# Turning attention probabilities by VectorE blocks and SBUF-to-SBUF DMAs instead of TensorE transposes

## The reference

```python
# layer 0
q, k, v = x @ Wq + bq, x @ Wk + bk, x @ Wv + bv          # split in 8 heads of 32
scores = einsum('bhnd,bhmd->bhnm', q, k) / sqrt(32)
attn = softmax(where(adj == 0, -inf, scores))
h = (attn @ v) @ Wo + bo
x1 = layernorm(h + x) * gamma0 + beta0
# layer 1
q, k, v = x1 @ Wq.T + bq, x1 @ Wk.T + bk, x1 @ Wv.T + bv
pros = softmax(where(adj == 0, -16384, q @ k.T))
z = v
for _ in range(4):
    z = 0.9 * (pros @ z) + 0.1 * v
out = layernorm(x1 + z) * gamma1 + beta1
```

## Time and profile before

| | us |
|---|---|
| runs of the kernel, median of 3 | 783.72 |
| lowest and highest | 782.49, 789.61 |
| the profiled execution, its time | 786.14 |
| its span, first to last instruction | 784.0 |
| PE busy | 754.1 (96%) |
| ACT busy | 665.7 (85%) |
| DVE busy | 637.1 (81%) |
| POOL busy | 547.8 (70%) |
| DMA, share of 16 engines (main queue) | 13.8% |

### The profile page before, as it was taken

How to read it: one execution, slowest core, us unless ns; L and a number is a source line. 1 busy time by engine, 2 the same in 40 slices (tenths; PEclk the granted TensorE clock), 3 DMA queues, 4 the chain that set the end, 5 groups by cost and what they waited for, 6 DMA issues and landing times.

```text
span 784.0 us, 32528 instructions
## 1 busy us (share of the span) xinstructions
PE 754.1 (96%) x11544; PEld 710.6 (91%) x11544; DVE 637.1 (81%) x3093; ACT 665.7 (85%) x2570; POOL 547.8 (70%) x417
## 2 busy tenths in 40 slices
PE   6889999999999999999999999999999999999974
PEld 6778999999999999999999999999999999998863
DVE  5778888888888888888888888888888888887765
ACT  4779998889889988988998898998889899899661
POOL 0336858666777777777787777787777778768774
PEclk9899999999999999999999999999999999999997
DMA  7101011010111101111111011111001111100002
GB/s 239 48 21 50 23 35 37 22 30 23 50 50 49 50 29 26 47 50 49 50 49 30 23 51 50 49 49 50 29 23 50 50 50 36 30 16 17 29 15 68
DMA packets 33245, 34.12 MB, mean 44 GB/s; under 512 B 2368, under 2 KB 28864, under 8 KB 33088
## 3 DMA queue, kind: packets, MB, share of 16 engines
q1 hardware_dynamic: 33088, 32.06, 13.8%
HBM read 23.67 MB, written 8.39 MB: 41 GB/s over the span
## 4 chain that ended last, share of the span: by engine, by line
PE 89%; DVE 3%; ACT 2%; issue 2%; DMA 1%; SPq 1%; POOL 1%; POOLq 0%; DVEq 0%; ACTq 0%
PE psF L342 23%; PE psF L411 18%; PE psF L351 16%; PE psF L401 15%; PE psS L391 9%; PE psF L456 7%; PE psF L436 2%; ACT ex L1011 2%; DMA w_raw<-in_w 1%; DVE sm L1400 1%; DMA out<-o_t 1%; SPq L284 0%; DVE o_t L1491 0%; DVE bst L1450 0%; POOL o_t L1927 0%
## 5 line engine op out<-in xcount | busy, mean ns | idle before, releaser
L1011 ACT ACTIVATE ex<-sm,nmax 128x128 f32<-128x128 f32 x1024 | 397.9, 397 | 3.3 <-DVE nmax L1400 2.3
L1859 POOL TENSOR_TENSOR pr<-ex,rec 128x1024 f32<-128x1024 f32 x128 | 245.3, 1918 | 101.1 <-DVE rec L1409 101.1
L1400 DVE CUSTOM_DVE_ANT_0 sm<-psS,mask 128x128 f32<-128x128 f32 x1024 | 228.3, 284 | 41.6 <-PE psS L391 41.4
L1011 ACT ACTIVATION_READ_ACCUMULATOR ex<-sm,nmax 128x1 f32 x1024 | 200.7, 196 | 0.0
L1022 ACT ACTIVATE pT<-psF 128x512 f32<-128x512 f32 x256 | 138.8, 596 | 34.5 <-PE psF L401 34.4
L401 PE MATMUL psF<-ident,pr 128*128 128x128 f32 x1024 | 137.8, 276 | 0.8 <-ACT pT L1022 0.5
L401 PEld LDWEIGHTS psF<-ident,pr 128*128 128x128 f32 x1024 | 112.7, 141 | 9.3 <-ACT pT L1022 0.9
L342 PE MATMUL psF<-xh,w_hi 128*128 128x256 f32 x512 | 112.6, 302 | 7.7 <-DVE w_lo L1339 5.7
L411 PE MATMUL psF<-pT,z 128*32 128x128 f32 x3072 | 103.1, 276 | 2.3 <-DVE z L1512 2.0
L342 PE MATMUL psF<-xh,w_lo 128*128 128x256 f32 x512 | 104.1, 285 | 0.0
L342 PE MATMUL psF<-xl,w_hi 128*128 128x256 f32 x512 | 103.6, 284 | 0.0
(11 more groups left out here) (76 smaller groups left out, 1425.7 us busy)
## 6 DMA issues: line engine op xcount, KB each, us to landing
xt_in<-in_x_t SPq DMA_DIRECT2D x32, 256.0 KB, 3.0
x_in<-in_x SPq DMA_DIRECT2D x32, 256.0 KB, 3.0
out<-o_t SPq DMA_DIRECT2D x30, 256.0 KB, 2.2
adj_in<-in_adj SPq DMA_DIRECT2D x32, 128.0 KB, 2.4
pT<-in_w SPq DMA_DIRECT2D x4, 256.0 KB, 4.0
row<-in_rows SPq DMA_DIRECT2D x1, 768.0 KB, 6.8
w_raw<-in_w SPq DMA_DIRECT2D x3, 256.0 KB, 7.0
out<-o_t SPq DMA_DIRECT2D x4, 128.0 KB, 1.7
```

The costliest lines, as they stand in the source:

```text
L1011: e = nc.scalar.activation(ex[l][:, b, h, :], sm[l][:, b, h, :], ACT.Exp, scale=-1.0, bias=nmax[l][:, b, h:h + 1], accum_out=tot[l][:, b, ...
L1400: last = nc.vector.tensor_tensor_reduce(sm[l][:, b, h, :], psS[:, o:o + N], mask[p.parity][:, b, :], -1.0, BIG, ALU.add, ALU.min, nmax[l][ ...
L1859: nc.gpsimd.tensor_tensor(pr[l][:, b, :, :], ex[l][:, b, :, :], rec[l][:, b, :].unsqueeze(2).broadcast_to([128, H, N]), ALU.mult).then_inc ...
```

## The change

DVE turns the probabilities in blocks of 32x32 (`turn_blocks`: one instruction for each layer and graph, 128 x 1024 each, from `ex` to the new tile `blk`). That leaves each block transposed in place, on the partitions of its row block; SP then carries block (i, j) to the partitions of column block j with 16 DMAs for each layer and pair (`move_blocks`), SBUF to SBUF. PE's `turn_probs`, ACT's `save_pT` and the tile `pr` are gone. POOL multiplies in place in `ex`.

With it: `save_q` and `save_k` go from DVE to ACT, as two ACTIVATE instructions of 128 x 256 each because ACT takes a bias of one column; hop 0's copy goes from DVE to ACT; the mask is kept four deep; the PSUM banks are dealt to other uses; `spread` reads the turned probabilities in runs of 32 elements. The orders of all engines are new, and the unrolled step runs from t = 9 to 31. POOL has waits on DVE's progress between its calls (`beside`), which guard no data.

```diff
-        mask = [sb(f"mask{i}", [128, 2, N]) for i in range(2)]
+        mask = [sb(f"mask{i}", [128, 2, N]) for i in range(4)]
-        pr = [sb(f"pr{l}", [128, 2, H, N]) for l in range(2)]
+        blk = [sb(f"blk{l}", [128, 2, NB, H, BS]) for l in range(2)]
-        pT0 = sb("pT0", [128, 2, H, N])
-        pT1 = [sb(f"pT1_{i}", [128, 2, H, N]) for i in range(2)]
+        pT0 = sb("pT0", [128, 2, NB, H, BS])
+        pT1 = [sb(f"pT1_{i}", [128, 2, NB, H, BS]) for i in range(2)]
...
+            def move_blocks(l, p):
+                if p.real:
+                    for b in range(2):
+                        sp.wait_ge(blk_s[l][b].sem, blk_s[l][b].at(p))
+                    if l:
+                        sp.wait_ge(hr[NUM_HOP - 1].sem, hr[NUM_HOP - 1].at(p - 2))
+                    else:
+                        sp.wait_ge(avr.sem, avr.at(p - 1))
+                    for i in range(NB):
+                        for j in range(NB):
+                            sp.dma_start(pT[l][p.parity][BS * j:BS * j + BS, :, i, :, :],
+                                         blk[l][BS * i:BS * i + BS, :, j, :, :]).then_inc(moved_s[l].sem, 16)
...
             def step(t):          # SP
-                load_xt(t + 2)
+                load_xt(t)
+                load_x(t - 2)
+                move_blocks(1, t - 5)
+                load_adj(t)
                 store(t - 9)
-                load_x(t + 1)
-                load_adj(t + 2)
+                move_blocks(0, t - 1)
...
-            def turn_probs(l, b, c, p):          # PE
-                    pe.wait_ge(pr_s[l][b].sem, pr_s[l][b].at(p))
-                    for g in range(G):
-                        last = nc.tensor.transpose(ps_T[l][b][c][:, g * N:(g + 1) * N], pr[l][:, b, G * c + g, :],
-                                                   ident[:, :])
...
             def spread(p_T, dst, src, done):
-                                                    p_T[:, b, h, :], start=True, stop=True)
+                                                    p_T[:, b, :, h, :], start=True, stop=True)
...
+            def save_q(l, p):          # ACT
+                    for c in range(C):
+                        bias = b1_col[:, 0, c:c + 1] if l else bq0s[:, c:c + 1]
+                        last = nc.scalar.activation(qT[l][:, c, :], ps_q[l][:, c * T:(c + 1) * T], ACT.Identity,
+                                                    bias=bias, scale=1.0 if l else SCALE)
...
-            def save_pT(l, b, c, p):          # ACT
...
+            def turn_blocks(l, b, p):          # DVE
+                if p.real:
+                    dve.wait_ge(pr_s[l][b].sem, pr_s[l][b].at(p))
+                    dve.wait_ge(moved_s[l].sem, moved_s[l].at(p - 1))
+                    nc.vector.transpose(blk[l][:, b, :, :, :].rearrange("p j h c -> p h j c"),
+                                        ex[l][:, b, :, :].rearrange("p h (j c) -> p h j c", c=BS)
+                                        ).then_inc(blk_s[l][b].sem, 1)
...
             def step(t):          # DVE, new order
+                turn_blocks(1, 1, t - 5)
+                aggregate(1, t - 8)
+                add_hop(2, t - 7)
+                turn_blocks(1, 0, t - 5)
+                reciprocals(0, 1, t - 1)
+                mask_scores(1, 0, 1, t - 4)
...
+                save_y(t - 2)
+                turn_blocks(0, 1, t - 1)
+                turn_blocks(0, 0, t - 1)
...
+                make_mask(t)
...
             def step(t):          # PE, new order, the part around attend and hop 0
+                values(1, 1, t - 4)
+                values(0, 1, t - 1)
+                scores(1, t - 4)
+                attend(t - 2)
+                hop(3, t - 7)
+                hop(1, t - 6)
...
+                scores(0, t)
+                hop(0, t - 5)
+                hop(2, t - 6)
```

More of the change, by code:

```diff
@@ L14 @@
 HD = D // H
+BS = 32
+NB = N // BS
 G = 4
@@ L319, in _ @@
+            begin()
+            run(step, 9, PAIRS)
+            end()
             for p in (Q, R):
@@ L492, in begin @@
                 keys(0, 1, Pair(1))
+                queries(0, 1, Pair(1))
+                free((mx[0][0][1], Pair(0)))
+                scores(0, Pair(1))
                 free((q_s[0], Pair(1)))
@@ L536, in begin @@
[L536 to L548, removed]
@@ new lines, in begin @@
+                free((mx[0][0][1], Pair(6)))
+                scores(1, Pair(3))
+                free((k_s[1], Pair(3)))
+                values(1, 0, Pair(3))
+                values(0, 1, Pair(6))
+                values(1, 1, Pair(3))
+                free((z_s[0], Pair(1)))
+                hop(1, Pair(1))
+                free((z_s[2], Pair(0)))
+                hop(3, Pair(0))
+                free((v_s[1], Pair(3)))
+                attend(Pair(5))
+                free((hT_s[1], Pair(1)))
@@ new lines, in begin @@
+                free((k_s[0], Pair(7)))
+                queries(1, 0, Pair(4))
+                free((z_s[3], Pair(0)))
+                keys(1, 0, Pair(4))
+                free((mx[1][1][0], Pair(3)))
+                scores(0, Pair(7))
+                keys(1, 1, Pair(4))
+                queries(1, 1, Pair(4))
+                free((q_s[0], Pair(7)))
+                hop(0, Pair(2))
+                free((z_s[1], Pair(1)))
+                hop(2, Pair(1))
+                free((k_s[1], Pair(4)))
@@ new lines, in begin @@
+                values(1, 0, Pair(4))
+                values(1, 1, Pair(4))
+                free((mx[0][1][0], Pair(7)))
+                scores(1, Pair(4))
+                free((q_s[1], Pair(4)))
+                turn_hop(0, Pair(2))
+                free((hT_s[2], Pair(1)))
+                turn_hop(2, Pair(1))
+                free((hT_s[0], Pair(2)))
+                values(0, 0, Pair(7))
+                values(0, 1, Pair(7))
+                free((v_s[1], Pair(4)))
+                attend(Pair(6))
@@ L805, in end @@
[L805 to L817 removed]
+                hop(3, Pair(25))
@@ L969, in _ @@
             begin()
-            run(step, 7, PAIRS)
+            run(step, 9, PAIRS)
             end()
@@ new lines, in begin @@
+                exp_two(1, 1, 1, 0, Pair(2))
+                save_q(1, Pair(3))
+                exp_two(1, 0, 0, 0, Pair(2))
+                exp_two(1, 1, 0, 0, Pair(2))
+                save_hop(2, Pair(0))
+                save_hop(0, Pair(1))
+                exp_two(0, 1, 0, 0, Pair(6), masked=True, turned=True)
+                save_k(1, Pair(3))
+                exp_two(0, 1, 0, 1, Pair(6))
+                exp_two(0, 1, 1, 0, Pair(6), masked=True)
+                exp_two(0, 1, 1, 1, Pair(6))
@@ new lines, in begin @@
+                exp_two(1, 0, 1, 1, Pair(4))
+                save_q(0, Pair(8))
+                exp_two(1, 0, 0, 0, Pair(4))
+                exp_two(1, 1, 1, 0, Pair(4), masked=True)
+                exp_two(1, 1, 1, 1, Pair(4))
+                save_q(1, Pair(5))
+                save_k(1, Pair(5))
+                save_hop(0, Pair(3))
+                save_hop(2, Pair(2))
+                exp_two(0, 1, 1, 1, Pair(8), masked=True, turned=True)
+                exp_two(0, 1, 0, 0, Pair(8), masked=True)
@@ L1852, in _, with beside @@
             pool.wait_ge(mh_s, 1)
+            def beside(done, p):
+                if p.real and not (done in on_s and p.last_two):
+                    pool.wait_ge(done.sem, done.at(p))
             def probabilities(l, b, p):
@@ L2045, in end @@
+                beside(ve_s[1], Pair(31) + 1)
                 shift_out(Pair(31))
             begin()
-            run(step, 7, PAIRS)
+            run(step, 9, PAIRS)
             end()
```

1981 lines of the change are left out of this document (1031 added, 950 removed).

## The result

The changed kernel takes 961.14 us (median of 4 runs, 959.63 to 967.14) against 785.26 us for the kernel before in the same set (4 runs). The ratio is 1.225, with a 95% interval of 1.217 to 1.233: slower by 22%, where the forecast was 744 us and the range 715 to 790. One of the 12 runs of experiment 12 (896.49 us, at a granted clock of 0.679) was in a slower state and does not enter its ratio.

The account below looks back on a forecast made before the run. PE was taken as the bound before, DVE after, at 21.5 us a step; fill 144, 25 steps 537.5 and drain 62.5 us gave a 744.0 us span, forecast 744 us against the median, range 715 to 790.

Parts of the forecast that it names:

- The bound before: In the kernel before, PE is the bound, busy for all 22.96 us of a steady step.
- steps of PE and ACT: Per steady step, PE falls from 22.96 to 19.7 us and ACT from 20.56 to 20.1 us.
- The step of DVE: Per steady step, DVE goes from 19.23 to 20.8 us and becomes the longest engine.
- The 0.7 us of idle time that the forecast allowed for: DVE's idle time in a step, kept for handoffs: a fifth of 3.73 us, making the step 21.5 us.
- The block transpose: On DVE, each 128x1024 block transpose costs 1.15 us, so four make 4.6 us a step.
- Rivals 1: DVE's transposes cost less, so a step takes 20.4 us and the kernel 716.5 us; chance 0.15.
- 3: DVE's transposes run at half rate, 2.2 us each, a step of 25.5 us and 844 us in all; chance 0.11.
- rival 5: In PE's matmuls, runs of 32 halve the moving operand's rate: PE 25.1 us a step, 834 us; chance 0.03.
- I take 0.43 us, because a move has a quarter of a load's bytes: On SP's queue, each issue takes 0.43 us, so 36 issues make 15.5 us a step.
- rival 4: SP's issue is the bound: at 0.65 us, 36 issues make 23.3 us a step, 789 us; chance 0.08.
- hides behind other pairs' work: In a step, each half of the moves, 6.9 us of issues plus 2.2 us landing, hides given most of a step.
- the clock, too, which the forecast had at 1.00: In the new steps, TensorE's granted clock stays at 1.00, with PE idle for under 2 of 21.5 us.

Follow-up runs that it names:

- experiment 12: experiment 11 with POOL's `add_bias` moved ahead of `shift_out`: 784.01 us, ratio 0.997 to the kernel before.
- experiment 1: The changed kernel with 16 moves of a layer and pair replaced by 4 straight 128-partition copies, same bytes, output not the attention's: 738.65 us, ratio 0.942.
- experiment 4: The kernel before with only turned probabilities laid out in runs of 32 elements: 783.65 us, ratio 1.001.
- experiment 5: The changed kernel with both graphs of a block side by side and each move cut from 64 KB to 4 KB: 933.13 us in one run.
- experiment 2: The changed kernel with three buffers instead of two for layer 1's turned probabilities: 878.83 us, ratio 1.123 to the kernel before.
- experiment 10: The changed kernel with flat blocks, three layer-1 buffers and eight single moves on ACT's queue, fill and drain included: 774.97 us, ratio 0.989 to the kernel before.
- experiment 11: experiment 10 with two short POOL calls moved ahead of layer 0's first multiplication: 776.88 us, ratio 0.991 to the kernel before.

## Why the prediction was wrong

**The bound before, and the steps of PE and ACT: right. The step of DVE: right in its sum, partly by luck.** With SP's issues cut to a quarter and all else kept, the kernel takes 738.65 us against the forecast of 744, with a mean step of 21.26 us against 21.5. In the stretch of experiment 1 PE is busy for 19.58 us (19.7 forecast) and ACT for 19.67 (20.1). For DVE a stretch of 22 steps is the better measure; the first row is of the changed kernel, the second of experiment 1:

```profile
211.43:837.50 626.07, 482.09 (x7216) 457.80 (x7216) 440.12 (x2090) 445.52 (x1785) 374.63 (x286) 0.88 0.44 108
167.88:635.65 467.77, 432.05 (x7216) 408.16 (x7216) 466.54 (x2092) 440.42 (x1786) 385.43 (x288) 1.00 0.46 145
```

DVE's own work is 440.12 / 22 = 20.0 us a step (20.8 forecast). In experiment 1 it is busy for 21.2 of 21.26 us, but 1.6 us of that is a subtraction that POOL held up, which no term of the forecast held (2.3 us on average in place of 0.7); the rest is 19.6 us. The 0.7 us of idle time that the forecast allowed for did not come. So the work was put 1.2 us too high, the idle time 0.7 too high and the subtraction 1.6 too low, and the three cancelled to within 0.3 us; the near hit on the step is in part luck. The block transpose occupies DVE for 1.145 us: two of them from 518.69, the next instruction at 520.98 (1.15 forecast).

```profile
518.69 2.36 DVE L1447 STREAM_TRANSPOSE blk<-ex 128x1024 f32<-128x1024 f32 x2
520.98 0.65 DVE L1550 TENSOR_TENSOR z<-psF,z0s 128x512 f32<-128x512 f32 x1
```

That is the rate of DVE's other rows, 1.04 ns an element and 0.08 us fixed. The Trainium skill's "Vector Engine (DVE) Microarchitecture Reference", section 3.8, has the transposing front end sustain one element per cycle per lane, and the trace agrees with it, since the transposes ran at the rate of the other instructions. Taking the 311 ns of the Trainium skill's "VectorE: DVE Perf Modes", section "The three transpose paths", and multiplying by size was wrong here: eight such squares in one instruction take 1.145 us in place of the 2.5 of that estimate. Rivals 1 and 3 are out by the price of the transpose, rival 5 by experiment 4.

**The step that failed: "I take 0.43 us, because a move has a quarter of a load's bytes".** The measured price is 0.65 us from start to start, and bytes have hardly anything to do with it (experiments 1 and 5). The row that carried the right number, three loads in 1.94 us, was read as a pile-up of data and used for rival 4 with a chance of 0.08. All rows of before were transfers between HBM and SBUF; none went from SBUF to SBUF, so the size argument had no row under it, and the range ought to have taken in both ends, as the prediction did for the block transpose.

**And the size of rival 4 was wrong as well.** It gave 789 us for 0.65 us an issue, by adding up SP's queue. The forecast said that each half of the moves "hides behind other pairs' work", and looked at each half alone. It even named what queues behind `move_blocks(1)`, but did not follow the waits round: SP waits for hop 3, hop 3 stands behind `attend` in PE's order, `attend` waits for the last move of layer 0, and that one is issued behind layer 1's 16 moves. The loop's length is 22.2 us of issues, 2.02 us of landing, 3.67 us of PE at the lower clock and 0.26 us of handoffs, 28.15 in all. Two such groups in a row at a granted clock of 1.00 take 1.95 us in the same step (524.75 to 526.70), so the clock, too, which the forecast had at 1.00, adds some 1.7 us to the loop. Cutting it with a third buffer gave 82 us back (experiment 2). Together: a step of 28.46 instead of 21.5 us makes 7.0 x 25 = 174 us of the 214 us between forecast and measured span (744.0 and 957.8); the rest is fill and drain, where the relay waits for the same issues; sharing them out there was worth 22 us in experiment 10.

**What stays open.** Why an issue from SBUF to SBUF costs 0.59 us and a load 0.34 to 0.47 us is not shown; the runs exclude bytes, partitions, and for the most part the number of runs. The kind of transfer is not shown as the reason either: a load issued right behind a move takes 0.58 us too and the one behind it 0.45 (rows of experiment 2), so part of the price may hang on what was issued just before. A version with half of the issues (both layers' blocks in one DMA) needs the attention moved by half a step on all engines and was not tried. Nor was the version of experiment 10 with its orders worked out for the new queues; its steady step is at 21.5 us, against 21.26 in experiment 1, so it is mainly fill and drain that separate it from 738 us.

## What to carry to other kernels

Before work is handed to DMAs, multiply their number by an issue time measured for the same kind of transfer, and where there is none, take the worst row as seriously as the best: here 32 issues of 0.65 us outweighed 3.3 us of TensorE transposes. Then follow the waits of the issuing queue all the way round, because an in-order queue that serves two consumers can turn a buffer's release into a loop that every issue lengthens. Here issues could be shared out to a busy compute engine's queue, one at a time between its instructions, and hardly cost it anything (0.4 us a step for eight); in groups of four they did (6.3 us for sixteen).

## What the runs showed of the hardware

An issue from SBUF to SBUF took 0.51 us at least and 0.59 to 0.63 us in the median, for 4, 64 and 256 KB, on SP's queue. On ACT's it took 0.61 to 0.62 us in groups of four and 0.52 alone. Landing took 1.7 us for 4 KB, 2.0 for 64 KB and 3.1 for 256 KB.

A VectorE subtraction of two SBUF tiles took 2.40 us beside a POOL multiplication and 0.70 without. In experiment 1 it began at 421.11, POOL's multiplication ran from 421.06 to 422.96, and POOL's next, short one was stretched to 1.75 us from 1.30:

```profile
421.06 1.90 POOL L1958 TENSOR_TENSOR ex<-ex,rec 128x1024 f32<-128x1024 f32 x1
422.91 1.75 POOL L1979 TENSOR_TENSOR xb<-x_in,bo_row 128x512 f32<-128x512 f32 x1
```

These lengths fit two instructions that take turns: the subtraction ended 0.55 us after POOL's multiplication did, and POOL's next one took 0.45 us longer than alone. By the Trainium skill, "SBUF — State Buffer", section "SBUF: two separate sides", the port pair that DVE and GpSimd share is an exclusive lock for a whole instruction, with which these rows agree. DVE's add of a PSUM and an SBUF tile was not held up: in experiment 11 it took 0.69 us (the row at 445.55) beside a POOL multiplication that began at 445.42. Reading the moving operand of a matmul in runs of 32 elements cost nothing (1.08 us a group of 32 either way), and after a pause of 5.33 us TensorE's next such group took 1.94 us, at a granted clock of 0.50.
